# Masking the first block on TensorE and reordering GpSimd, VectorE and SyncE work in a fused graph-attention and mixture-of-experts kernel

## What is computed

```python
h  = layernorm(x)
lQ, lK, lV = masked_x @ Wlq, h @ Wlk, h @ Wlv + blv
scores = where(adj, lQ @ lK.T / 16, -1e9)
# two more weights per row: a global one (gQ, gK, gV from the mean of h) and an extra one (es, eV)
res = softmax_over(scores, global, extra) @ (lV, gV, eV)
x1  = x + maximum(res, masked_x)
n   = layernorm(x1)                       # then normed again with ln_g, ln_b
xa  = normed @ attn_w.T + attn_b + n
y   = expert_e(xa)                        # 8 experts, 512 tokens each: fc1, gelu, fc2
out = x1 + gelu(y @ next_w.T + next_b)
```

## Time and profile before

| what | value |
|---|---|
| median of 3 runs | 1088.6 us (1088.25 to 1088.91) |
| the profiled execution | 1089.44 us |
| its span, first to last instruction | 1087.6 us |
| mean granted TensorE clock, share of full speed | 0.992 |
| busy, share of the span: TensorE, VectorE, GpSimd, ScalarE | 96%, 79%, 65%, 50% |
| scoring of the first block starts | 18.8 us |
| first tile of block 0 centred | 105.0 us |
| final block weighed beside the first expert's start | about 738 to 808 us |

### The profile page before, as it was taken

How to read it: one execution, slowest core, us unless ns; L and a number is a source line. 1 busy time by engine, 2 the same in 40 slices (tenths; PEclk the granted TensorE clock), 3 DMA queues, 4 the chain that set the end, 5 groups by cost and what they waited for, 6 DMA issues and landing times.

```text
span 1087.6 us, 15808 instructions
## 1 busy us (share of the span) xinstructions
PE 1041.1 (96%) x4996; PEld 869.1 (80%) x4996; DVE 856.1 (79%) x1532; ACT 542.9 (50%) x974; POOL 706.8 (65%) x717
## 2 busy tenths in 40 slices
PE   6878999999999999999999999999798999999998
PEld 5656887887887888788788788887687888888886
DVE  5889887797898789879879978987876775577653
ACT  5541444444444445344444444448566555655664
POOL 5764776777678677676767767768475455554451
PEclk9999999999999999999999999999899999999999
DMA  7585343453354345345425425449936647654621
GB/s 224 187 285 182 118 152 109 159 174 103 121 181 136 125 160 175 102 141 182 131 100 175 165 97 169 146 138 352 333 102 212 210 148 245 224 175 150 208 78 59
DMA packets 104341, 180.39 MB, mean 166 GB/s; under 512 B 14265, under 2 KB 45882, under 8 KB 104002
## 3 DMA queue, kind: packets, MB, share of 16 engines
q1 hardware_dynamic: 104258, 179.38, 49.2%
HBM read 143.63 MB, written 27.33 MB: 157 GB/s over the span
## 4 chain that ended last, share of the span: by engine, by line
PE 80%; DVE 6%; POOL 5%; issue 3%; DMA 3%; ACT 2%; SPq 1%; DVEq 0%; POOLq 0%; ACTq 0%
PE u_ps L1579 19%; PE s_ps L52 11%; PE s_ps L54 11%; PE s_ps L53 11%; PE u_ps L1586 9%; PE u_ps L52 2%; PE u_ps L54 2%; PE u_ps L53 2%; PE mt_ps L52 2%; PE mt_ps L53 2%; PE mt_ps L54 2%; POOL p_lo L713 2%; POOL m_lo L774 1%; PE mb_ps L52 1%; PE mb_ps L53 1%
## 5 line engine op out<-in xcount | busy, mean ns | idle before, releaser
L713 POOL TENSOR_TENSOR p_lo<-p_all,p_hi 128x512 fp32r<-128x512 f32 x224 | 295.7, 1320 | 172.1 <-PE u_ps L1586 104.9
L1309 ACT ACTIVATE p_hi<-scores 128x512 fp32r<-128x512 f32 x224 | 141.6, 632 | 358.8 <-DVE scores L886 358.5
L902 DVE TENSOR_TENSOR scores<-s_ps,bias 128x512 f32<-128x512 f32 x256 | 175.5, 686 | 85.5 <-PE s_ps L54 82.0
L1579 PE MATMUL u_ps<-p_hi,v_in 128*128 128x512 f32 x896 | 241.0, 391 | 0.0
L52 PE MATMUL s_ps<-q_hi,lnT_hi 128*128 128x512 f32 x512 | 202.5, 396 | 11.4 <-DVE scores L902 10.0
L53 PE MATMUL s_ps<-q_lo,lnT_hi 128*128 128x512 f32 x512 | 200.8, 392 | 0.0
L54 PE MATMUL s_ps<-q_hi,lnT_lo 128*128 128x512 f32 x512 | 200.7, 392 | 0.0
L1579 PEld LDWEIGHTS u_ps<-p_hi,v_in 128*128 128x128 f32 x896 | 167.2, 188 | 34.0
L705 POOL TENSOR_SCALAR bias<-adj 128x512 f32<-128x512 uint8 x256 | 164.9, 645 | 15.7 <-DVE scores L902 15.7
L886 DVE TENSOR_TENSOR scores<-scores,mb_ps 128x512 f32<-128x512 f32 x256 | 171.7, 676 | 0.8 <-PE mb_ps L1604 0.8
L923 DVE TENSOR_TENSOR kept_ps<-kept_ps,scores 128x512 f32<-128x512 f32 x232 | 162.2, 699 | 8.0
(11 more groups left out here) (216 smaller groups left out, 1770.9 us busy)
## 6 DMA issues: line engine op xcount, KB each, us to landing
v_in<-v_scratch SPq DMA_DIRECT2D x118, 512.0 KB, 3.6
adj<-in_adj SPq DMA_DIRECT2D x64, 256.0 KB, 3.9
raw<-in_wffn SPq DMA_DIRECT2D x32, 512.0 KB, 5.2
v_scratch<-vst SPq DMA_DIRECT2D x8, 1024.0 KB, 6.0
mx<-in_mx SPq DMA_DIRECT2D x18, 256.0 KB, 6.8
xg<-in_x SPq DMA_DIRECT2D x8, 512.0 KB, 4.6
uhi_scratch<-uT_high SPq DMA_DIRECT2D x8, 512.0 KB, 2.7
ulo_scratch<-uT_low SPq DMA_DIRECT2D x8, 512.0 KB, 3.6
```

The lines of the kernel that those rows point to most:

```text
L713: nc.gpsimd.tensor_tensor(out=low_part(y), in0=whole_part(y), in1=high_part(y).bitcast(fp32), op=ALU.subtract).then_inc(plo_ready, 1)
L902: nc.vector.tensor_tensor(scores[:, t % SLOTS], s_ps[t % 3][:, :], bias[:, t % 2], ALU.add).then_inc(masked, 1)
L1309: nc.scalar.activation(high_part(y), scores[:, y % SLOTS], ACT.Exp, scale=SCALE).then_inc(phi_ready, 1)
L1579: nc.tensor.matmul(u_ps[d][:, :], values[:, x % 2, at:at + P], high_part(x), start=k == 0 and part == 0, stop=False)
```

## The change

The change has four parts.

1. **First block's mask.** `bias_of(t)` for t < 32 writes a tile `turned_bias` in fp32r (in the place of `bias`), and TensorE adds it to the scores with a seventh matmul by an identity matrix, `ident_high`. VectorE's `mask` for these tiles is gone. In its place ScalarE copies the masked tile from the bank to the ring (`keep_score`). The masked value becomes -2**34, which fp32r holds exactly. `score(t)` now also waits for the bias tile, and `bias_of(t)` for the score two tiles back.
2. **Order in the first block.** GpSimd makes `bias_of(t+2)` and `bias_of(t+3)` ahead of the first `low_values`, `bias_of(t+4)` between the two, and `bias_of(t+5)` ahead of `reciprocal_deviation`; `low_weight_matrix(0)` and `(1)` move from g = 0 to g = 2. VectorE makes `low_turned` ahead of `keep` from group 2 on. ScalarE does `normalise` in two halves with a `keep_score` between. SyncE issues `load_masked(1)` ahead of its wait for `low_values` of group 0 instead of behind it. The third load of values waits for the last score of block 0.
3. **Query inputs of every later block.** ScalarE's rounding moves from k = 22 to 21, GpSimd's two halves from k = 23 and 24 to 22 and 23.
4. **Final block.** Tiles 15, 18 and 21 are no longer late, so GpSimd makes their low parts. `normalise(0, 1)` moves from i = 13 to 14, `low_normed(0, 0)` from 16 to 15, `shares` of block 6 from 15 to 17 and the store of its coefficients from 16 to 18, `shares` of block 7 from j = 3 to j = 4 of the first expert.

```diff
-MASKED = -1.0e9 / SCALE
+MASKED = -float(2 ** 34)
@@ is_late
-            return y >= LAST + 4 and y % 3 == 2
+            return y >= LAST + 4 and y % 3 == 2 and y - LAST not in (15, 18, 21)
@@ SyncE, group(g)
+                    if g == 1:
+                        sp.wait_ge(q_done, 2)
+                        load_masked(sp, 1)
                     if g > 0:
                         sp.wait_ge(vlo_ready, 2 * g)
                         sp.dma_start(v_dram[(g - 1) * TG:g * TG]...
-                    if g == 1:
-                        sp.wait_ge(q_done, 2)
-                        load_masked(sp, 1)
@@ SyncE
                 for i in range(VRING):
+                    if i == VRING - 1:
+                        sp.wait_ge(score_done, KT)
                     load_values(sp, i)
...
-                    ended = ended_since(t, 8, 16)
+                    ended = ended_since(t, 8, 18)
@@ GpSimd
-                    wait(pool, masked, t - 1)
-                    nc.gpsimd.tensor_scalar(bias[:, t % 2], adj8[...], -MASKED, MASKED, ...
+                    wait(pool, score_done if t < KT else masked, t - 1)
+                    nc.gpsimd.tensor_scalar(turned_bias[:, t % 2] if t < KT else bias[:, t % 2], adj8[...], -MASKED, MASKED, ...
...
                         bias_of(t + 2)
+                        bias_of(t + 3)
                     if g < NG:
                         low_values(g, 0)
                     if g > 0:
-                        bias_of(t + 3)
+                        bias_of(t + 4)
                     if g < NG:
                         low_values(g, 1)
-                    if g > 0:
-                        bias_of(t + 4)
+                    if 0 < g < NG:
+                        bias_of(t + 5)
                     if 0 < g and g + 2 < NG:
                         reciprocal_deviation(g + 2)
-                    if 0 < g < NG:
-                        bias_of(t + 5)
-                    if g == 0:
+                    if g == 2:
                         low_weight_matrix(0)
                         low_weight_matrix(1)
...
-                    if k in (23, 24) and n + 1 < BLOCKS:
-                        low_queries_input(n + 1, k - 23)
+                    if k in (22, 23) and n + 1 < BLOCKS:
+                        low_queries_input(n + 1, k - 22)
@@ VectorE
-                    if i in (12, 13):
-                        normalise(0, i - 12)
-                    if i == 16:
+                    if i in (12, 14):
+                        normalise(0, (i - 12) // 2)
+                    if i == 15:
                         low_normed(0, 0)
...
-                        if e == 0 and j == 3:
+                        if e == 0 and j == 4:
                             shares(BLOCKS - 1)
...
+                        if i == 0 and g == 1:
+                            shift(g + 1)
+                        if i == 0 and 1 < g < NG:
+                            low_turned(g, 0)
+                            low_turned(g, 1)
                         if g > 0:
-                            mask(t + i)
                             keep(t + i)
-                        if i == 0 and g < NG:
-                            if 0 < g and g + 1 < NG:
-                                shift(g + 1)
+                        if i == 0 and 1 < g and g + 1 < NG:
+                            shift(g + 1)
+                        if i == (1 if g == 1 else 0) and g < 2:
                             for k in range(KD):
                                 low_turned(g, k)
...
-                    ended = ended_since(t, 6, 15)
+                    ended = ended_since(t, 6, 17)
@@ ScalarE
+                def keep_score(t):
+                    act.wait_ge(score_done, t + 1)
...
+                    nc.scalar.activation(scores[:, t], s_ps[t % 3][:, :], ACT.Copy).then_inc(masked, 1)
...
                 for g in range(NG):
+                    t = 4 * g - 4
+                    if g > 1:
+                        keep_score(t - 1)
+                    if g == 1:
+                        keep_score(0)
+                        keep_score(1)
                     (lnT_hi of group g, two copies)
+                    if g > 1:
+                        keep_score(t)
                     if g + 1 < NG:
-                        normalise(g + 1)
+                        normalise(g + 1, range(2))
+                    if g > 1:
+                        keep_score(t + 1)
+                    if g + 1 < NG:
+                        normalise(g + 1, range(2, TG))
...
+                    if g > 0:
+                        keep_score(t + 2)
+                for t in range(KT - 5, KT):
+                    keep_score(t)
...
-                    if k == 22 and n + 1 < BLOCKS:
+                    if k == 21 and n + 1 < BLOCKS:
                         high_queries_input(n + 1)
@@ TensorE, score(t)
+                    if t < KT and t % 4 == 0:
+                        pe.wait_ge(tlo_ready, t // 2 + 2)
...
+                    if t < KT:
+                        pe.wait_ge(bias_ready, t + 1)
+                        pe.wait_ge(ident_high_ready, 1)
+                        last = nc.tensor.matmul(s_ps[t % 3][:, :], ident_high[:, :], turned_bias[:, t % 2], start=False, stop=True)
+                    last.then_inc(score_done, 1)
```

More of the change, by code:

```diff
@@ L137, in gnn_moe_kernel @@
         bias = rings("bias", [P, 2, CH])
+        turned_bias = nc.alloc_sbuf_tensor_at("turned_bias", [P, 2, CH], fp32r, offset=q_at + 8 * SLOT + 4 * CH * 2)
         mxt = rings("mxt", [P, D])
@@ L213, in gnn_moe_kernel @@
         vst = before("vst", [P, 2, TG, 2 * D], fp32r)
+        ident_high = before("ident_high", [P, P], fp32r)
         def masked_parts(n):
@@ L274, in gnn_moe_kernel @@
         phi_ready, pall_ready, plo_ready, pv_done = (sem(n) for n in ("phi_ready", "pall_ready", "plo_ready", "pv_done"))
-        late_low_ready = sem("late_low_ready")
+        late_low_ready, ident_high_ready = sem("late_low_ready"), sem("ident_high_ready")
         bev_placed = sem("bev_placed")
@@ L703, in bias_of @@
                         pool.wait_ge(adj_in[g % 2], 16 * (g // 2) + 16)
-                    wait(pool, masked, t - 1)
-                    nc.gpsimd.tensor_scalar(bias[:, t % 2], adj8[:, t // 4 % 2, t % 4 * CH:(t % 4 + 1) * CH], -MASKED, MASKED,
+                    wait(pool, score_done if t < KT else masked, t - 1)
+                    nc.gpsimd.tensor_scalar(turned_bias[:, t % 2] if t < KT else bias[:, t % 2], adj8[:, t // 4 % 2, t % 4 * CH:(t % 4 + 1) * CH], -MASKED, MASKED,
                                             ALU.mult, ALU.add).then_inc(bias_ready, 1)
@@ L890, in mask @@
                     dve.wait_ge(bias_ready, t + 1)
[L891 to L894, removed]
                     if t == 32:
@@ L1467, in expert, with normalise @@
                         nc.scalar.activation(y_hi[:, k], y_ps[k][:, :], ACT.Identity, bias=b2_c[:, 2 * e + k:2 * e + k + 1]).then_inc(yhi_ready, 1)
-                def normalise(g):
+                def keep_score(t):
+                    act.wait_ge(score_done, t + 1)
+                    if t == 16:
+                        act.wait_ge(wlo_ready, 4)
+                    if t == 20:
+                        act.wait_ge(w_stored, 32)
+                    nc.scalar.activation(scores[:, t], s_ps[t % 3][:, :], ACT.Copy).then_inc(masked, 1)
+                def normalise(g, tiles=range(TG)):
                     act.wait_ge(nmr_ready, g + 1)
@@ L1474, in normalise @@
                     wait(act, vlo_ready, 2 * g - 2)
-                    for j in range(TG):
+                    for j in tiles:
                         last = nc.scalar.activation(lnf[g % 2][:, j, 1:D], xg[:, g % 2, j, 1:D], ACT.Identity, scale=rstd[:, g % 2, j:j + 1],
                                                     bias=nmr[:, g % 2, j:j + 1])
-                    last.then_inc(ln_ready, 1)
+                    if TG - 1 in tiles:
+                        last.then_inc(ln_ready, 1)
                 def high_values(g):
@@ L1488, in _ @@
                 high_queries_input(0)
+                act.wait_ge(ident_ready, 2)
+                nc.scalar.activation(ident_high[:, :], ident[:, :], ACT.Copy).then_inc(ident_high_ready, 1)
                 normalise(0)
@@ L1560, in score @@
                     wait(pe, masked, t - 2)
+                    if t < KT and t % 4 == 0:
+                        pe.wait_ge(tlo_ready, t // 2 + 2)
                     ks = slice(k * P, (k + 1) * P)
-                    split_product(nc, s_ps[t % 3][:, :], [(lnT_hi[:, d, ks], lnT_lo[:, d, ks]) for d in range(KD)],
-                                  [(q_hi[:, n % 2, d], q_lo[:, n % 2, d]) for d in range(KD)]).then_inc(score_done, 1)
+                    last = split_product(nc, s_ps[t % 3][:, :], [(lnT_hi[:, d, ks], lnT_lo[:, d, ks]) for d in range(KD)],
+                                         [(q_hi[:, n % 2, d], q_lo[:, n % 2, d]) for d in range(KD)], stop=t >= KT)
+                    if t < KT:
```

(1 more changed line is left out.)

## The result

| | before | after |
|---|---|---|
| median of 4 runs | 1088.76 us (1088.25 to 1089.6) | 1081.57 us (1080.43 to 1083.81) |
| ratio, 95% interval | | 0.9936 (0.9919 to 0.9953) |
| profiled execution, its span | 1089.44, 1087.6 us | 1083.81, 1081.6 us |

A forecast was written before the change was run, and what follows sets the result against it. TensorE was busy 96% of the span, but in the first block a chain round the engines was taken to bound. 6.1 + 4.6 + 2.9 - 1.2 = 12.4 off 1089.44 gave 1077.0, median 1076; range 1068 to 1085.

The forecast's parts named there:

- First block, 6.1: First block: 3.5 us gained up to the last normalise, and net 2.6 from there to the first centred tile.
- 33.5: First block: normalise(3) would start at 33.5 instead of 37.45, with the query input loaded earlier.
- 8.8 + 0.6 - 0.4 = 9.0: First block, one group: 8.8 us before, plus 0.6 for keep_score, minus 0.4 for shift no longer behind a mask.
- The tail, 26.6 forecast: First block's end, to the first centred tile: 29.2 us before, eight masks shed 5.4, 2.8 given back, net 2.6.
- bias(6), 3.2 + 1.5: First block, group 2 to 3: TensorE stalls 3.2 us for bias(6), then 7 matmuls at half clock cost 1.5.
- Unknown prices: First block: fp32r bias taken as 0.62 us, identity matmul 0.23, keep_score 0.58; all dear, it loses about 5 us.
- Query inputs, 4.6: Blocks 2 to 7: rounding a step earlier removes TensorE's six waits for m_lo, 4.6 us, ends 3.5 and 4.6.
- Final block, 2.9: Before attend(0, 0): 3.7 us of VectorE work moves away, minus 0.8 for contention; 2.9 gained, ends 1 and 5.5.
- the 0.8 for contention: Final block: one more VectorE instruction slowed beside GpSimd's subtractions costs 0.8 to 1.0 us, taken as 0.8.
- First expert, -1.2: First expert: shares of block 7 later delays store, tokens and TensorE by 1.2 us, ends -1.5 and +1.
- the cycle eats the first block's gain: First block rival: each keep_score waits for GpSimd, adding 0.9 to 1.2 us in six groups; 1082, chance 0.15.
- The rival of the final block: Final block gives nothing, as GpSimd holds VectorE: 1079, chance 0.10.

The follow-up runs named there:

- the move of the reciprocal: Kernel after with GpSimd's reciprocal deviation ahead of the second low value and bias(t+5) in groups 1 to 5: 1081.54 us, 0.9931.
- query_inputs_alone: Kernel before with only the query inputs of blocks 2 to 7 rounded one step earlier: 1083.07 us, 0.9938.
- the repeat of after: Kernel after, unchanged, run again beside the kernel before: 1081.51 us, 0.9931.
- nt_lo_earlier: Kernel after with VectorE's low part of the first half's normalised tokens ahead of the second half's normalise: 1079.1 us, 0.991.
- final_block_alone: Kernel before with the final block's order alone, without the move of shares of block 7: 1088.33 us, 0.999.

## Why the forecast was too high, step by step

- **First block, 6.1.** Measured: nothing, 1.0003, and 1.3 in the trace. Taking the constant out by difference (1.0033), the rest of the edits are worth 3.3 us, if the two add; the intervals leave about 1.8 us on either side. Of the 4.8 us between 6.1 and 1.3, three steps account. The early load of the input came as forecast (no wait for it on ScalarE in after), but normalise(3) came 2.4 us later after normalise(1) than forecast: 33.5 was worked out without contention, and nmr took 1.23 us beside GpSimd's subtraction, the second low value 1.77. The group's 8.8 + 0.6 - 0.4 = 9.0 is 9.32, 0.6 in the last two: `shift` no longer waits behind a `mask`, but for GpSimd, so its 0.4 came to nothing, while two biases bring 4 x 0.12 of distance. With the change in, the cycle runs through GpSimd, as the move of the reciprocal shows. The tail, 26.6 forecast, was 28.5, so 1.9: the copies stand 1.6 us apart on ScalarE, each waiting for TensorE. (The two groups between them cancel out, 0.5 each way.) Also wrong: my starts were anchored at before's clock. They matched raw times only because that execution began 1.75 us earlier.
- **bias(6), 3.2 + 1.5.** The stall came (3.30, and the clock fell: 0.83 granted from 34 to 44), but taking it away gave 0.3, not its length, and the half clock, 1.5 in the forecast, cost nothing measurable.
- **Unknown prices.** turned_bias 0.62, as taken; `keep_score` 0.57 to 0.61, as taken. The price that I did not ask for was the changed constant.
- **Query inputs, 4.6.** Right in kind, and too small: 6.7 by the part alone (5.2 to 8.3). In after, 5.4 us come between the first centred tile and the first late weighing, against 6.3 in query_inputs_alone. The wait for m_lo is gone in both, but the new constant still takes 0.2 us a block (90.9 to 91.1 against 90.7).
- **Final block, 2.9.** Measured 1.1. The mis-sized term is the 0.8 for contention. xf, 1.70 in the earlier trace rows and again for the second half, took 2.62, and xn, 0.72 before, took 2.15:

```profile
764.85 2.15 DVE L1034 TENSOR_SCALAR xn<-x_next,cmv,crstd 128x256 f32<-128x256 f32 x2
...
766.92 2.62 DVE L1034 TENSOR_SCALAR xf<-x_next,cmv,crstd 128x256 f32<-128x256 f32 x2
```

```profile
763.02 7.65 POOL L717 TENSOR_TENSOR low_scores<-scores,p_late 128x512 fp32r<-128x512 f32 x6
```

GpSimd now had six subtractions in a row there, and VectorE lost 1.4 + 0.9 = 2.3 us on these two pairs alone. From the start of this xn to nT_lo it needed 5.81 us, 6.84 before: 3.4 less work and 2.3 of contention. The first half's xf fell from 1.70 to 0.73, but that brought nothing, as the second xn starts 33.0 us after the first late weighing in both. The Trainium skill ("SBUF — State Buffer", section "SBUF: two separate sides") gave nothing for this part; the row of before, one contention of 0.8, gave too much. The measured 1.1 lies between, nearer to the page's.
- **First expert, -1.2.** The wait for mT grew as forecast, from 2.43 to 3.63 and 2.90 us. But what the expert loses or gains hangs on the clock after the stall for h_lo, and the repeat of after shows the experts at the time of before (256.2 against 256.3).
- **Luck.** The range holds the result in part by luck: the query inputs gave 2.1 us more than forecast, while the first block gave nothing of its 6.1, and in the repeat of after the experts took the time of before, not 1.2 more.
- **Rivals.** The time is that of "the cycle eats the first block's gain" (1082), and the cycle did grow. Its mechanism was half right: what lengthened the ring was GpSimd, not ScalarE's order alone. The rival of the final block came in part.

Left open: what makes 6.7 of 4.6 in the queries, where the constant's other 2 us go, whether the clock is what decides the wait in the second expert, and how after would run with the old constant, which was not tried.

## What to carry to other kernels

Compare traces from a common event, not from the span's start, and repeat the profile before a stall is called the kernel's. Before an edit that lightens one engine, follow the ring once around and add up the engine that closes it; here GpSimd closed it 0.3 us a group above the forecast. Ask too what runs beside each link: a 0.16 us instruction took 1.23 here. Small moves that can't be told from noise one by one can be judged together, 6.9 us here; that the sum is more than its parts these runs don't show.

## What was not expected of the hardware

- The constant of a GpSimd instruction (-2^34 for -1.6e10) adds 0.12 us ahead of it and 0.05 to 0.12 behind it, with the instruction's own 0.62 us unchanged. With the one constant changed the kernel took 3.6 us more.
- A clock drop may save time (the pairing is seen, the cause is not set): with TensorE at 1.2 GHz after a stall of 2.68 us, the next stall was 0.45 us; at 2.4 GHz after one of 3.41 us, it was 3.16. A stall of over 3 us did not always lower the clock: the 3.3 us for bias(6) did in after and not in nt_lo_earlier.
- The clock may fall at one place in one execution and not in another of the same code there: near 94 us in final_block_alone (0.74 granted from 92 to 98.5), not in before, 1.6 us of the span.
- The same VectorE instruction pair (xf) took 0.73, 1.70 or 2.77 us, with no, one or two GpSimd operations on 128x512 tiles beside it. The tiny nmr took 1.23 us beside one and 0.16 without.
